# B rows broadcast by transfers instead of TensorE in three of four rows, the scan's input formed in SBUF, eight shared PSUM banks, and the norm's totals folded into the residual add

## The reference: what is computed

```python
x = x + attention(layernorm(x))                 # 16 heads, chunks of 64, feature maps, head norm
x = x + mixer(ctx, z=layernorm(x))              # below
x = x + ffn(layernorm(x))                       # ternary weights, int8-like rows, 512 -> 2048 -> 512
# mixer: u (512 channels) from ctx by a projection, a 4-tap convolution, silu
#        dt, B, C from u; 16 states n for each channel
dA = jnp.exp(d[..., None] * A)
state = state * dA + (d * u)[..., None] * b[:, None, :]      # over 512 steps
y = jnp.einsum('bdn,bn->bd', state, c)
y = (y + D * u) * silu(z)
```

## Time and profile before

| what | value |
|---|---|
| median of 3 runs | 933.81 us (931.28 to 936.23) |
| profiled execution, its own time | 930.31 us |
| its span | 928.5 us |
| mean granted TensorE clock | 0.926 |
| busy: PE, DVE, ACT, POOL | 84%, 83%, 63%, 53% of the span |

### The profile page before, as it was taken

The page is one execution under the profiler, slowest core; times in us unless marked ns, Lnnn a source line. Parts: engine busy times, 40 slices in busy tenths (PEclk is TensorE's granted clock), DMA queues, the critical chain, the costliest instruction groups (busy, mean ns, idle before and its releaser), DMA issues. The chain is left out here.

```text
span 928.5 us, 11643 instructions
## 1 busy us (share of the span) xinstructions
PE 779.2 (84%) x4020; PEld 426.0 (46%) x4020; DVE 775.0 (83%) x955; ACT 584.7 (63%) x868; POOL 488.4 (53%) x292
## 2 busy tenths in 40 slices
PE   5759898359597879998987888997889899998798
PEld 1334555243363334665453334655446335664243
DVE  5877788995989985988589988689788998987875
ACT  3788899974756956546266876363456786453453
POOL 0457688786656623675346644276454745574020
PEclk9789998679989998989989999998998999999799
DMA  8688789767545634757535663456653565775000
GB/s 289 255 243 233 226 246 257 226 186 178 114 102 118 121 74 97 169 130 172 112 68 118 132 125 68 126 119 149 148 115 83 120 130 119 159 153 119 1 12 35
DMA packets 50782, 131.12 MB, mean 141 GB/s; under 512 B 7298, under 2 KB 7874, under 8 KB 50724
## 3 DMA queue, kind: packets, MB, share of 16 engines
q0 software_dynamic: 16128, 58.73, 33.6%
q1 hardware_dynamic: 34596, 71.65, 23.9%
HBM read 67.09 MB, written 4.35 MB: 77 GB/s over the span
## 5 line engine op out<-in xcount | busy, mean ns | idle before, releaser
L1709 POOL TENSOR_TENSOR W<-W,CROW 128x1024 f32<-128x1024 f32 x128 | 321.6, 2529 | 157.0 <-DVE W L1898 132.0
L1898 DVE TENSOR_TENSOR_SCAN W<-DEC,PB 128x1024 f32<-128x1024 f32 x125 | 285.1, 2281 | 9.2 <-issue 3.0
L1722 POOL DMA_DIRECT2D ACC<-W x112 | 98.3, 878 | 153.0 <-DMA ACC<-W 130.4
L1887 DVE TENSOR_TENSOR PB<-DU,PB 128x1024 f32<-128x1024 f32 x128 | 156.5, 1223 | 17.1 <-PE PB L1043 13.6
L1332 ACT ACTIVATE DEC<-DT,ACOL 128x511 f32<-128x511 f32 x250 | 160.1, 710 | 9.8 <-DVE W L1898 9.6
L1096 PE MATMUL bank<-W,ARENA 128*128 128x512 fp8e4 x512 | 125.0, 388 | 0.0
L1287 ACT ACTIVATE ARENA<-bank 128x512 f32<-128x512 f32 x56 | 32.5, 591 | 72.9 <-PE bank L868 35.4
L1096 PEld LDWEIGHTS bank<-W,ARENA 128*128 128x128 bf16 x512 | 45.5, 99 | 62.7 <-issue 19.0
L1430 ACT ACTIVATE ARENA<-bank,SDQ 128x512 f32<-128x512 f32 x64 | 43.3, 686 | 45.0 <-PE bank L1096 44.8
L1043 PE MATMUL PB<-BC,ID 96*128 96x512 bf16 x98 | 38.5, 410 | 29.6 <-DVE W L1898 28.1
L2040 DVE SCALAR_TENSOR_TENSOR ARENA<-bank,SDQ,ARENA 128x512 f32<-128x512 f32 x64 | 47.4, 743 | 17.4 <-PE bank L1096 6.8
(11 more groups left out here) (177 smaller groups left out, 1320.5 us busy)
## 6 DMA issues: line engine op xcount, KB each, us to landing
ACC<-W POOLq DMA_DIRECT2D x112, 512.0 KB, 4.6
CROW<-c_rows SPq DMA_DIRECT2D x98, 256.0 KB, 3.5
W<-in_wffn SPq DMA_DIRECT2D x27, 512.0 KB, 6.0
X<-in_wffn SPq DMA_DIRECT2D x21, 512.0 KB, 5.1
X<-in_x SPq DMA_DIRECT2D x7, 1024.0 KB, 8.0
out_dram<-X SPq DMA_DIRECT2D x16, 256.0 KB, 2.1
X<-in_ctxT SPq DMA_DIRECT2D x4, 512.0 KB, 5.6
ARENA<-in_x SPq DMA_DIRECT2D x1, 1024.0 KB, 6.2
```

Source lines behind the costliest of these rows:

```text
L1709: pool.tensor_tensor(w, w, CROW[k % 2][:, :].unsqueeze(1).broadcast_to([P, 2, L]), ALU.mult)\
L1722: pool.dma_start(ACC[accumulator(u)][:, :, :], w, accum_op=ALU.add).then_inc(y_summed, 16)
L1887: dve.tensor_tensor(into, du, rows, ALU.mult).then_inc(dbu_done.sem, 1)
L1898: dve.tensor_tensor_scan(flat(W[u % 4]), flat(decay_of(u)), flat(PB[:, scan_bank(u):scan_bank(u) + 2, :]), 0.0, ALU.mult, ALU.add).then_in ...
```

## The change

1. In rows 1 to 3, SP loads row n of B onto all partitions (`b_row`, into two new SBUF buffers `BRW`) from `bc_rows` in DRAM, where B and C are now stored together. PE's spreads, the cut of B, and its transfers remain for row 0 alone.
2. In rows 1 to 3 DVE forms the product of a unit in `W[u % 4]`, from `DU` and `BRW`, both in SBUF; the scan reads `DEC` and that `W` and writes over it. The wait for room in `W` moves from the scan to the product (`room`).
3. The three banks of `PB` join the five common ones after row 0's last scan.
4. The residual add also gives its row total (`TOTALS`); the mean comes from it by a [128 x 1] operation (`mixer_mean`), the sum of squares from a new ACT operation (`deviations`), in place of the statistics operations of DVE.
5. `normed` uses another form of instruction, in which the scale is a second SBUF tensor.
6. All tables of places hold other numbers. Small tensors share allocations.

```diff
-    def __init__(self, ctx, nc, name, count, products):
-        self.banks = [ctx.enter_context(nc.psum_tensor(f"{name}{k}", [P, 512], fp32)) for k in range(count)]
+    def __init__(self, ctx, nc, name, own, lent, lent_free, products):
+        self.banks = [ctx.enter_context(nc.psum_tensor(f"{name}{k}", [P, 512], fp32)) for k in range(own)] + lent
+        self.lent, self.lent_free, count = own, lent_free, own + len(lent)
...
     def free_at(self, *key):
         k, r = self.place[key]
+        if k >= self.lent and r == 0:
+            return self.lent_free
         return self.drained_sem[k], r
...
+        if b == 1:
+            every, four, last = (*every, *five_on), (*every, *five_on)[:-1], (*every, *five_on)[-1:]
         out += on(every, [(f, "yT", t) for t in range(TT)])
...
+    [(('r', 0), 3), (('r', 1), 0), (('r', 2), 1), (('c', 0, 1), 3), (('c', 0, 2), 0), (('c', 0, 3), 1),
...
-SPLIT_AFTER = (9, 25, 25, 0)
+B_AHEAD = 3
...
-        ID96 = sb("ID96", [96, 32], bf16)
...
-        EPSC = sb("EPSC", [P, 1])
...
+        BRW = [sb(f"BRW{i}", [P, L]) for i in range(2)]
...
+        BC3 = BRW[1][0:96, 0:L // 2].bitcast(bf16)
+        ID96 = BRW[1][0:96, L // 2:L // 2 + 16].bitcast(bf16)
...
+        R = Banks(ctx, nc, "bank", 5, [PB[:, i, :] for i in range(LENT)], scan_done.at(0), all_products())
...
-                sp.dma_start(CROW[k % 2][:, :], c_rows[b, n].partition_broadcast(P)).then_inc(c_loaded[k % 2].sem, 16)
...
+                sp.dma_start(CROW[k % 2][:, :], bc_rows[b, N + n].partition_broadcast(P))\
+                  .then_inc(c_loaded[k % 2].sem, 16)
...
+            def b_row(u):
...
+                b, _, n = unit(u)
+                k = SPREAD_OF[u]
+                if u % UNITS == 0:
+                    sp.wait_ge(*bc_stored.at(b))
+                if SPREAD_OF[u] < UNITS + 2:
+                    sp.wait_ge(*b_bcast.at(0))
+                else:
+                    sp.wait_ge(*dbu_done.at(0, LAST_WITH[k - 2] + 1))
+                sp.dma_start(BRW[k % 2][:, :], bc_rows[b, n].partition_broadcast(P)).then_inc(b_loaded[k % 2].sem, 16)
...
+            def store_rows(b):
                 sp.wait_ge(*R.drained_at(b, "xdbl"))
-                sp.dma_start(c_rows[b], XBC[N:2 * N, :]).then_inc(c_stored.sem, 16)
...
+                sp.dma_start(bc_rows[b], XBC[0:2 * N, :]).then_inc(bc_stored.sem, 16)
...
             for j in range(-1, UNITS):
-                if j + 2 == UNITS:
-                    store_c(1)
+                if j + B_AHEAD == UNITS:
+                    store_rows(1)
+                b_row(j + B_AHEAD)
                 if j >= 0:
                     c_row(j + 2)
-                if j == SPLIT_AFTER[0] + 2:
-                    split_rows(1)
...
+                    b_row(b * UNITS + j + B_AHEAD)
                     if b * UNITS + j + 2 < TOTAL:
                         c_row(b * UNITS + j + 2)
...
-                if u % UNITS == 0:
+                if u == 0:
                     pe.wait_ge(*bc_parts.at(b))
-                pe.matmul(PB[:, 2 * (k % 2), :], ID96[:, n:n + 1].broadcast_to([96, P]), BC3[b % 2][:, :],
+                pe.matmul(PB[:, 2 * (k % 2), :], ID96[:, n:n + 1].broadcast_to([96, P]), BC3,
                           start=True, stop=True).then_inc(b_bcast.sem, 1)
...
                 for u in spreads_at(b, point):
-                    if not joined(u):
+                    if u < UNITS:
                         spread_b(u)
...
+            def deviations(f, t):
+                act.wait_ge(*mean_ready.at(f, t + 1))
+                act.activation(Z[:, t, :], X1[:, t, :], ACT.Square, bias=NMEAN[:, t:t + 1],
+                               accum_out=LNV[1][:, t:t + 1]).then_inc(var_ready.sem, 1)
...
+                if i == 1:
+                    act.wait_ge(*var_ready.at(b))
+                    act.activation(LNV[1][:, :], LNV[1][:, :], ACT.Ln, bias=EPSC[:, :], scale=1.0 / D)\
+                       .then_inc(ln_log[i].sem, 1)
+                else:
...
-                if b:
-                    act.wait_ge(*R.full_at(b, "xdbl"))
-                    act.activation(BC3[b % 2][0:2 * N, :], R.bank(b, "xdbl")[0:2 * N, :], ACT.Copy)\
-                       .then_inc(split_cut.sem, 1)
                 drain((b, "xdbl"), XBC[:, :], R.bank(b, "xdbl")[0:2 * N + RANK, :])
...
+                for t in range(TT):
+                    deviations(f, t)
                 rstd(f, 1)
...
-            def split(b):
-                first, whole = BC3[b % 2][0:32, :], XBC[0:32, :]
-                pool.wait_ge(*R.drained_at(b, "xdbl"))
-                pool.wait_ge(*split_cut.at(b - 1))
-                pool.tensor_tensor(BCR, whole, first, ALU.subtract).then_inc(split_step.sem, 1)
-                pool.wait_ge(*split_step.at(b, 1))
-                pool.tensor_copy(BC2, BCR).then_inc(split_step.sem, 1)
-                pool.wait_ge(*split_step.at(b, 2))
-                pool.tensor_tensor(BC1, BCR, BC2, ALU.subtract).then_inc(split_step.sem, 2)
             for e in range(KT):
...
+                    dve.scalar_tensor_tensor(XROWS[b][:, t, :], XROWS[b][:, t, :], MV[0][:, t, 0:1],
+                                             RSTD[0][:, t:t + 1].broadcast_to([P, D]), ALU.subtract, ALU.mult)\
+                       .then_inc(xn_ready.sem, 1)
             def normed_peak(f, t):
...
+            def room(u):
+                if u - 4 < PAIRED and u % 2 == 0:
+                    dve.wait_ge(pair_added, (u - 4) // 2 + 1)
+                else:
+                    dve.wait_ge(y_summed, 16 * transfers(u - 4))
...
             def inputs_b(u):
                 b, h, n = unit(u)
-                if u:
-                    dve.wait_ge(*scan_done.at(0, u))
-                if not joined(u):
-                    dve.wait_ge(*b_bcast.at(0, SPREAD_OF[u] + 1))
+                k = SPREAD_OF[u]
                 if opens(u):
                     dve.wait_ge(*du_ready.at(b, 2 * h + 2))
-                rows = PB[:, 2 * (SPREAD_OF[u] % 2), :].unsqueeze(1).broadcast_to([P, 2, L])
-                if scan_bank(u):
-                    into, du = PB[:, 1:3, :], DU[:, 2 * h:2 * h + 2, :]
+                if b:
+                    room(u)
+                    dve.wait_ge(*b_loaded[k % 2].at(0, 16 * (k // 2 + 1 - UNITS // 2)))
+                    rows, into, du = BRW[k % 2][:, :], W[u % 4][:, :, :], DU[:, 2 * h:2 * h + 2, :]
                 else:
-                    into, du = PB[:, 1::-1, :], DU[:, 2 * h + 1:2 * h - 1 if h else None:-1, :]
-                dve.tensor_tensor(into, du, rows, ALU.mult).then_inc(dbu_done.sem, 1)
+                    if u:
+                        dve.wait_ge(*scan_done.at(0, u))
+                    dve.wait_ge(*b_bcast.at(0, u + 1))
+                    rows = PB[:, 2 * (k % 2), :]
+                    if scan_bank(u):
+                        into, du = PB[:, 1:3, :], DU[:, 2 * h:2 * h + 2, :]
+                    else:
+                        into, du = PB[:, 1::-1, :], DU[:, 2 * h + 1:2 * h - 1 if h else None:-1, :]
+                dve.tensor_tensor(into, du, rows.unsqueeze(1).broadcast_to([P, 2, L]), ALU.mult)\
+                   .then_inc(dbu_done.sem, 1)
             def scan(u):
                 dve.wait_ge(*dbu_done.at(0, u + 1))
                 dve.wait_ge(*da_ready.at(0, u + 1))
-                if u >= 4:
-                    if u - 4 < PAIRED and u % 2 == 0:
-                        dve.wait_ge(pair_added, (u - 4) // 2 + 1)
-                    else:
-                        dve.wait_ge(y_summed, 16 * transfers(u - 4))
-                dve.tensor_tensor_scan(flat(W[u % 4]), flat(decay_of(u)), flat(PB[:, scan_bank(u):scan_bank(u) + 2, :]), 0.0,
+                if u < UNITS:
+                    if u >= 4:
+                        room(u)
+                    inputs = PB[:, scan_bank(u):scan_bank(u) + 2, :]
+                else:
+                    inputs = W[u % 4]
+                dve.tensor_tensor_scan(flat(W[u % 4]), flat(decay_of(u)), flat(inputs), 0.0,
                                        ALU.mult, ALU.add).then_inc(scan_done.sem, 1)
...
                    .then_inc(R.drained(f, "yT", t), 1)
-            def mixer_sums(f, t):
+            def mixer_mean(f, t):
                 dve.wait_ge(*R.drained_at(f, "wo", t))
-                sums(f, 1, X1, t)
...
-                mixer_sums(f, 2)
+                mixer_mean(f, 2)
                 units(b, "v", 2)
-                mixer_sums(f, 3)
+                mixer_mean(f, 3)
                 units(b, "v", 3)
-                aggregate(f, 1)
                 gate_shift(f)
                 units(b, "r", 3)
                 units(b, "r", 4)
```

More of the change, by code:

```diff
@@ L184, in ffn_products, with last_products @@
     return out
-def last_products(f):
+def last_products(f, every):
     out = [((f, "wo", 0), (0,)), ((f, "ms", GROUPS - 1), (3,))] + [((f, "wo", t), (t,)) for t in range(1, TT)]
@@ L200, in last_products @@
     row += [(f, "hT", TT - 1, j) for j in range(HC)] + [(f, "O", TT - 1)]
```

(43 more changed lines are left out.)

84 lines of the change are left out of this document (35 added, 49 removed), and 225 rows, old and new, of tables (STEP_DECAYS, STEP_PIECES, STEP_SPREADS).

## The result

The changed kernel takes **1017.3 us** in the median (1015.0 to 1021.5), the kernel before 933.5 in the same comparison: ratio 1.090, 95% interval [1.086, 1.094], or +84 us. The forecast was +56. The profiled execution took 1019.2 us, 1017.4 of it the span.

What follows compares the result with a forecast made beforehand. No engine bounds alone: DVE and PE wait for each other in turn. 139 + 10 - 7 - 6 - 80 = +56 on 930.3 us gives 986, plus 3.5 for the median: 990 us; own range 955 to 1015, wider 940 to 1028.

Steps and rivals of the forecast that it cites:

- Stalls, +139 and +10: Steps 1 to 3: DVE's product and scan exclude POOL's multiplication, +139 us (0 to 230), and its other operations, +10 (0 to 29).
- the count over the order: New DVE order, 96 scans: one-input operations hide 91 of 230 us, leaving 139 us of stalls; old order also 139.
- What DVE's idle time absorbs, -80: Steps 1 to 3: PE catches up during stalls, so most of DVE's 91 us of waits goes, -80 us (-45 to -91).
- The first rival: Steps 1 to 3: half of DVE's idle time stays, -45 in place of -80, 1025 us; chance 0.13.
- Totals and `normed`, -13: Steps 1 to 3: norm totals replacing statistics, -7 us (-9 to 0); new form of `normed`, -6 (-6 to 0).
- PE and the banks, 0: Steps 1 to 3: dropped spreads (27 us of PE) and eight banks are worth nothing by themselves.
- B's loads, 0: Rows 1 to 3: 66 loads land in about 3.5 us with 5.8 us available, so they cost 0.
- The fourth rival: SP queue: B's loads stand behind C's and come late, every second by 1.5 us, 1020 us; chance 0.08.
- Row 0, -4 to +3: Row 0 and the last row: products stay in PSUM, fewer statistics and more banks against squares, 0 us (-4 to +3).

Runs made afterwards that it cites:

- 7: Changed kernel, POOL in rows 1 to 3 filling W by memset instead of multiplying by C: 939.1 us, 1.000 of the kernel before.
- 1: Kernel before, product of rows 1 to 3 written into W, so only the scan has two SBUF inputs: 968.4 us, +33 (1.036).
- 9: Changed kernel with old tables, five common banks and the product of rows 1 to 3 formed in PSUM: 1008.8 us, +77 (1.082).
- 3: Changed kernel, POOL in rows 1 to 3 multiplying only one of a unit's two tiles by C: 961.1 us, +25 (1.030).
- 8: Control: kernel before, POOL in rows 1 to 3 filling W by memset instead of multiplying by C: 924.5 us, -18 (0.981).
- run 11: Kernel before with only the folded norm totals and the new form of `normed`: 936.7 us, +5 (1.005).
- run 12: Changed kernel, old tables, five banks, product in PSUM, memset for POOL's multiplication in rows 1 to 3: 955.1 us, +22 (1.024).

## Why the prediction came out as it did

The kernel is 9% slower where 6% was forecast. The mechanism, DVE's operations held by POOL's and POOL's by DVE's, was right; the cost came out too high, and what idle time takes of it far too high.

**Stalls, +139 and +10: right, a little high.** The collisions are what makes the kernel slower (7, and 1 and 9 for each operation), both operations collide, and a stall ends with POOL's instruction (3). Measured were 125 us, against 149: about 110 behind multiplications, where the count over the order gave 139, and about 15 behind the other operations, where the sum had 10. The sentence of the Trainium skill that the prediction weighed ("SBUF — State Buffer", Who interferes with whom) agrees with the trace in both directions, for operations of 1.2 to 4.8 us; that the first to start always goes first isn't so in every instance (last section).

**What DVE's idle time absorbs, -80: the step that failed most.** 34.6 us were absorbed in the steps, 27.5 over the run. Per us of stall the runs give 0.6 (1, the scan) and 0.6 (7 against 8) at the end, where the sum had (149 - 80)/149, under 0.5. The working took DVE's idle time as slack that PE fills by running ahead. But the waits go both ways: a stalled drain leaves PE without a bank, and its next product is late for DVE. The profile shows both halves, PE's idle time up by 56.6 us and DVE's waits for the scores as large as before (19.9 us for 19.2); that each late product follows from a stalled drain was not traced one by one. The first rival, with half absorbed, has this mechanism, and its 45 us is nearer to the measured 35. Its total, 1025 us, is nearer too. How much the lower granted clock (0.89 for 0.95) adds by itself was not tried; it can be effect or cause.

**Totals and `normed`, -13: wrong in sign**, +5 by run 11. `normed` was priced at 0.67 us against a mean of 1.23 before, but that mean holds the old form's waits for POOL; without them the old form takes 0.53 us and the new one 0.74, and both wait for POOL (11); in the changed kernel the group takes 14.7 us where it took 14.0. The totals' term had the small operations for the mean, but not the reads of the accumulator that come with them (1.3 us, half of the 32 small instructions of 11), and ACT's squares do stand on the path: the three waits for `RSTD` grew from 1.8 to 6.1 us.

**PE and the banks, 0: wrong.** -15 us with the old tables. This is the one part that gives time, and the new tables go with it: without the eight banks they cost 24 us.

**B's loads, 0: mis-sized.** Of 66 loads 62 are hidden, as worked out; four are not, for 10.6 us in the changed kernel. Two are the first of row 1, 8.0 us: store, fetch, and a load of weights ahead of both on SP's queue come one after the other. Rows 2 and 3 begin without such a wait. The other two, 2.7 us, and 9.6 of the 16.8 us in run 12, stand behind a store of finished output on SP's queue. The working took the load as issued once its buffer is free. The fourth rival saw that the queue can hold B up, but by the loads of C and for every second load, which isn't in the trace. **Row 0, -4 to +3: wrong**, it is +16.5 us. 7.0 are this wait, 4.4 are scans that wait longer for the transfer into `ACC` (7.2 us, 2.8 before), and 5.2 are row 0's eight operations of `normed` (12.6 us for 7.4), longer by themselves and held longer by POOL. Smaller differences of either sign were not traced.

The parts add up: with old tables and five banks the scan alone (+33) and the product with B and totals (+77) make 110, measured together +100; the banks take 15 off and the tables 1, which is +84. Of the 77, 37 vanish with POOL's reads (9 against 12, 55, less the control's 18, which is known to 10 us), and 40 remain. The waits for B (17), the totals (5) and what is left of stalls (14, at 0.6 some 8) are 30 of these, if each wait for B reaches the end whole, which wasn't tested; the other 10 are open. My +56 was 136 of work less 80; the chip's +89 is 116 of work less 27. Two errors of 20 and 53 us, in opposite directions, and the smaller hid a part of the larger: that the forecast came within 27 us of the time is partly luck.

No version run here is faster than the kernel before while it computes the same; the only part that gained, the banks, needs B out of PSUM, and that is what puts two inputs into SBUF.

## What to carry to other kernels

Before an operand is moved from PSUM to SBUF, list for every DVE operation that then reads two tensors from SBUF what POOL does at that time; count what is left of POOL's instruction as a stall, and also the reverse. Look for a queue that works in order: a load whose buffer is free still waits for what stands ahead of it (12). An engine's idle time inside a ring of waits (DVE drains for PE, PE computes for DVE) isn't slack: here a quarter to two fifths of the added stalls went into it. Tables of an order are tuned to the buffers they were made with: five banks instead of eight cost 15 us with the old tables and 40 with the new. That more buffers are worth more when an engine in the ring stutters was not shown: almost without stalls, run 12 (five banks, old tables) and run 7 (eight, new, and the scan's input in SBUF) lie 22 us apart, with stalls the same step is worth 16.
